# Attention stage: the copies of the transposed probabilities from PSUM to SBUF move from VectorE to ScalarE

## What is computed

```python
# x: (16, 2048, 1024), D_K = 128, D_FF = 4096
xn = _layernorm(x)
Q, K, V = xn @ Wq, xn @ Wk, xn @ Wv
logits = Q K^T * D_K ** (-0.5)          # causal mask above the diagonal: -inf
attn = softmax(logits)
a = (attn @ V) @ Wo
hidden = xn @ W1 + b1
q = hidden + (cos(th)*wr + sin(th)*wi) * (wi*sin(th + hidden*0.1)) * 0.1
f = relu(q) @ W2 + b2
x + a + f
```

## Time and profile before

| | |
|---|---|
| median of 2 runs | 1229.64 us (1228.83 to 1230.45) |
| profiled execution | 1230.11 us |
| its span on the slowest core (core 6), first to last instruction | 1228.5 us |
| spans of the eight cores | 1222.5 to 1228.5 us |
| busy: PE, ACT, DVE | 88%, 48%, 37% of the span |
| attention stage, first sequence | 71.9 to 132.9 us of the span |
| attention stage, second sequence | 192.6 to 267.4 us |
| FFN stage | from 268 us to the end; from 268 to 1225 us PE is busy for 928.9 of 957 us |
| the 80 copies L591 on DVE | 48.9 us busy |

### The profile page before, as it was taken

The page is one execution under the profiler, slowest core; times in us unless marked ns, Lnnn a source line. Parts: engine busy times, 40 slices in busy tenths (PEclk is TensorE's granted clock), DMA queues, the critical chain, the costliest instruction groups (busy, mean ns, idle before and its releaser), DMA issues.

```text
span 1228.5 us, 23871 instructions; the slowest of 8 cores (1222.5 to 1228.5 us)
## 1 busy us (share of the span) xinstructions
PE 1084.7 (88%) x7936; PEld 733.9 (60%) x7936; DVE 452.8 (37%) x1007; ACT 595.5 (48%) x1285; POOL 37.0 (3%) x48
## 2 busy tenths in 40 slices
PE   1767474769999999999999999999999999999998
PEld 1644373446566656665666566656665666566665
DVE  3626553643333333333333333333333333333333
ACT  2955494445454544454445444544454445444444
POOL 1310021000000000000000000000000000000000
PEclk9968686789999999999999999999999999999999
DMA  7889578920202020202020202020202020202000
GB/s 166 252 139 170 159 228 142 176 87 1 77 11 86 1 87 1 87 1 86 2 86 2 86 1 87 1 86 2 86 1 87 1 87 1 86 1 87 20 33 35
DMA packets 47416, 87.13 MB, mean 71 GB/s; under 512 B 7106, under 2 KB 23490, under 8 KB 46274
## 3 DMA queue, kind: packets, MB, share of 16 engines
q1 hardware_dynamic: 36226, 59.39, 15.8%
q0 software_dynamic: 11072, 26.22, 11.6%
HBM read 78.25 MB, written 25.17 MB: 84 GB/s over the span
## 4 chain that ended last, share of the span: by engine, by line
PE 72%; DVEq 2%; DVE 2%; issue 1%; ACT 1%; ACTq 0%
PE psOut L832 37%; PE psW L806 36%; DVEq L752 2%; DVE probs L754 1%; ACT rb_sb L779 1%; DVE u_sb L731 1%; DVE out_sb L754 0%; ACT L771 0%; DVEq L759 0%; DVEq L730 0%; ACT ss_sb L771 0%; DVEq L751 0%; DVEq L728 0%; ACTq L778 0%; ACTq L776 0%
## 5 line engine op out<-in xcount | busy, mean ns | idle before, releaser
L832 PE MATMUL psOut<-W_sb,rb_sb 128*128 128x512 bf16 x2048 | 532.5, 383 | 10.8 <-ACT rb_sb L779 10.8
L806 PE MATMUL psW<-xn_r,W_sb 128*128 128x256 bf16 x4096 | 537.5, 275 | 1.5 <-PEq L386 1.5
L806 PEld LDWEIGHTS psW<-xn_r,W_sb 128*128 128x128 bf16 x4096 | 404.0, 99 | 161.7 <-issue 6.2
L731 DVE SCALAR_TENSOR_TENSOR u_sb<-ss_sb,Rp_sb,psW 128x256 f32<-128x256 bf16 x512 | 244.2, 479 | 584.5 <-ACT ss_sb L771 571.2
L771 ACT ACTIVATE ss_sb<-psW,phb_sb 128x256 bf16<-128x256 f32 x512 | 242.4, 474 | 445.3 <-PE psW L806 445.3
L832 PEld LDWEIGHTS psOut<-W_sb,rb_sb 128*128 128x128 bf16 x2048 | 200.8, 99 | 151.8 <-issue 20.9
L779 ACT ACTIVATE rb_sb<-u_sb,b_sb 128x256 bf16<-128x256 f32 x511 | 254.5, 498 | 57.1 <-DVE u_sb L731 55.1
L591 DVE CAST pT_big<-psT 128x512 bf16<-128x512 f32 (+2 forms) x80 | 48.9, 612 | 38.6 <-PE psT L526 34.0
L370 PE MATMUL psTx<-diag_li,probs 128*128 128x128 bf16 x176 | 15.5, 239 | 41.0 <-DVE diag_li L274 40.8
L526 PE MATMUL psT<-diag_li,xn_rg 128*128 128x128 bf16 x272 | 31.8, 264 | 22.2 <-DVE pT_big L591 15.6
L540 PE MATMUL psO<-pT_big,V_tm 128*128 128x128 bf16 x272 | 30.8, 253 | 17.7 <-DVE pT_big L591 16.7
(11 more groups left out here) (92 smaller groups left out, 429.5 us busy)
## 6 DMA issues: line engine op xcount, KB each, us to landing
x_sb<-x SPq DMA_DIRECT2D x52, 512.0 KB, 6.0
W_sb<-w POOLq DMA_DIRECT2D x8, 2048.0 KB, 40.7
xn_scr<-xn_rg POOLq DMA_DIRECT2D x32, 256.0 KB, 4.3
xn_r<-xn_scr SPq DMA_DIRECT2D x16, 512.0 KB, 7.5
out<-out_sb SPq DMA_DIRECT2D x32, 256.0 KB, 3.1
out<-probs SPq DMA_DIRECT2D x32, 256.0 KB, 5.3
xn_r<-x SPq DMA_DIRECT2D x12, 512.0 KB, 6.4
Q_fm<-b2rep SPq DMA_DIRECT2D x1, 512.0 KB, 3.7
```

What stands on the lines that cost most here:

```text
L731: su2.inc(v.scalar_tensor_tensor(u2_sb[ci % 2][:], ss_sb[ci % 2][:], Rp_sb[:, c:c + 1], psW1[slot][:], ALU.mult, ALU.add))
L806: ins = t.matmul(psW1[slot][:], W1_sb[:, k * DFF + c * 128: k * DFF + (c + 1) * 128], xn_r3[g % 2][:, k * R3:(k + 1) * R3], start=(k == 0) ...
L832: ins = t.matmul(psOut[tt][:, h * 512:(h + 1) * 512], rb_sb[cw % 3][:, tt * 128:(tt + 1) * 128], W2_sb[:, cc * D + h * 512: cc * D + (h + ...
```

## The change

The copies leave DVE's loop and enter ACT's. On ACT they stand behind the exponentials of tile qi and ahead of the copy of psO, with the same waits but with no drain ahead of each. Their semaphores are the same. PE's program is unchanged.

```diff
@@ vector engine, attention stage
                         se2.inc(ins)
-                        for si in range(nsg[j]):
-                            b = bank_of[(j, si)]
-                            v.wait_ge(stx2.h, stx2_b + cum_sg[j] + si + 1)
-                            if j >= 1:
-                                v.wait_ge(spv.h, spv_b + j)
-                            v.drain()
-                            w = segw2(j, si)
-                            (st2e if b == 0 else st2eV).inc(v.tensor_copy(
-                                pT_big[si // 2][:, (si % 2) * 512:(si % 2) * 512 + w],
-                                psT2[b][:, 0:w]))
                         for fn in pv.get(j, []):
                             fn(v)
@@ scalar engine, attention stage (qq is the query tile, j = qq - 1)
                                 se1.inc(ins)
+                        if j >= 0:
+                            for si in range(nsg[j]):
+                                b = bank_of[(j, si)]
+                                sc.wait_ge(stx2.h, stx2_b + cum_sg[j] + si + 1)
+                                if j >= 1:
+                                    sc.wait_ge(spv.h, spv_b + j)
+                                w = segw2(j, si)
+                                (st2e if b == 0 else st2eV).inc(sc.copy(
+                                    pT_big[si // 2][:, (si % 2) * 512:(si % 2) * 512 + w],
+                                    psT2[b][:, 0:w]))
                         j2 = qq - 1
```

## The result

| | before | after |
|---|---|---|
| median of the runs beside each other | 1231.18 us (14 runs) | 1234.86 us (15 runs) |
| ratio after / before | | 1.0035, 95% interval 1.0026 to 1.0044 |
| span of the slowest core in the profile | 1228.5 us | 1235.0 us |

A forecast was written before the change was run, and what follows sets the result against it. It took a chain of handovers, with no engine full, to bound the attention stages. First sequence +5.6, second -2.0 and clock +2 on 1230.1 gave 1235.7, stated as 1235 us; range 1231 to 1239 (0.62), eight in ten 1227 to 1243.

The forecast's parts named there:

- Copies are late by the second exponential: First sequence, large tiles: copies on ACT start only after the next tile's second exponential; whole first sequence +5.6 us.
- the term for the place: First sequence, tiles 11 to 14: copies queued behind the exponentials lengthen the steps by +4.0 us in sum.
- A pitch of 0.47 us: Copies on ACT: successive 512-column copies start 0.47 us apart, against some 0.75 us on DVE.
- The two ACT copies of the earlier trace: Existing ACT copies of the same shape, type and memories, taken as the model: 0.60 us each, pitch 0.47.
- The bound of +6 us for a longer pitch: Copies on ACT: a pitch of 0.60 + 0.15 us instead of 0.47 would add +0.25 in some 24 steps, +6.
- Second sequence: diag_li early: Without copies DVE makes diag_li sooner; tiles 2 to 7 change by -3.6 us, the whole second sequence by -2.0.
- The stall is given back: Second sequence, tile 14: ACT's 4.2 us wait before the arctangent goes, but tile 13's later copies give it back almost whole.
- The clock, +2 us within 0 to 7: Attention stages, nine large steps: sparser PE work lowers its granted clock; +2 us taken, 7 if all fall, 0 if none.
- The faster copy wins: Rival, attention stages: shorter copies and vanished waits save 25 us, giving 1205; chance 0.02 whole, 0.13 for a mild gain.
- The clock stays low: Rival, tiles 9 to 15 of both stages: 0.8 us a tile, 7 in all, giving 1240.7; chance 0.18.
- a term that I had at 0: Layer norm stage between the two attention stages: forecast difference 0.

The follow-up runs named there:

- e3: Changed kernel, but for query tiles 8 to 15 the copies stand on ACT between the two exponentials; ratio to before 0.9969.
- e10: Kernel before, copies on DVE, but in the first sequence each tile's copies wait for the next tile's exponentials; ratio to before 1.0142.
- e8: Changed kernel with 12 unused matmuls on idle PE ahead of the third segment's transposes of tiles 8 to 15; ratio to before 0.9992.
- e4: Changed kernel with a drain put ahead of each copy on ACT, as DVE had; ratio to before 1.0102.
- e6: Kernel before with only DVE's step L460 of tile 13 moved ahead of that tile's copies; ratio to before 0.9970.

## Why the prediction was right

The measured 1234.86 us lies beside the 1235 forecast. The nearness is in part luck: the forecast was built on two runs of before with a median of 1229.64 us, and the median of the 14 runs is 1231.18. The difference was forecast as 5.6 us (5.4 from that median) and is 4.3 (3.2 to 5.4). The mechanism, late copies in the first sequence and earlier diag_li in the second, is as forecast. Point by point, by medians of the cores (medians of single steps do not add up exactly to the median of a stage):

- **Copies are late by the second exponential.** Right. Tile 12's first copy starts at its end (113.74) to the hundredth, and e3 and e10 show that the place is the cause. The steps of tiles 8 to 10 grew by 0.5, 0.6 and 0.0 us (+1.4 forecast for the three, 1.1 measured) and small tiles by +0.2 in all (+0.3). Tiles 11 to 14 grew by 4.8 us in all where the term for the place was 4.0; with the gaps filled (e8), at the clock of before (0.96 against 0.95), they grow by 2.9. So the place alone was put too high by about 1 us there, and the clock adds 1.9. The step of tile 12 on core 6 was to be near 5.1 us and is 5.43; the logits at 1.2 GHz make the difference and more.
- **A pitch of 0.47 us.** Right, 0.48; DVE's, put at 0.75, is 0.78. Since ACT's copies overlap, all 80 add 38.3 us to its busy time on core 6 and not 43. The two ACT copies of the earlier trace rows were the right neighbours. The bound of +6 us for a longer pitch was too small: with a drain (pitch 0.67), which also delays each first copy, it is 11 us (e4).
- **Second sequence: diag_li early.** Right to 0.1 us: tiles 2 to 7 (with the sliver of tiles 0 and 1) are 3.6 us shorter, as forecast. Tiles 8 to 11 came to +0.5 (0.5 forecast), 12 and 13 to +2.8 (2.0), 14 and the last to -1.8 (-0.9); the last two misses cancel.
- **The stall is given back.** Right. Two table loads and two exponentials now stand ahead of tile 13's copies; the step went from 8.94 to 8.74, and e6 shows the 3.7 us that could be had.
- **The clock, +2 us within 0 to 7.** Right in kind. e8 gets 4.0 us back in the two stages. That is more than the change itself lost by the clock, most likely: over the whole stages the granted clock, median of the cores, fell from 0.68 and 0.67 to 0.67 and 0.64 by the change, and the filling raised it to 0.75, above that of before.
- **The rivals.** "The faster copy wins" needs copies that do not wait for the exponentials. They did wait (e10), and of its 25 us (14.6 of them at 0.26 us a copy, where the two pitches of the prediction differ by 0.28) only the 3.6 of the small tiles in the second sequence, 0.2 at the arctangent and the shorter pitch came about. "The clock stays low" is a part of the truth and not the whole.
- **What no step foresaw**: the layer norm stage between the two, 0.8 to 1.4 us longer by the means over twelve profiles, 2.5 in the first pair.

The parts add up to what the timed runs give (3.2 to 5.4): +5.5 and -2.6 us from the attention stages and 0.8 to 1.4 from the layer norm stage make 3.7 to 4.3. The agreement is loose, since one profile of the first stage is good to about 2 us. The hit of the total owes something to luck here too: the attention stages alone gave 3 us where I had 5.6, and a term that I had at 0 filled a good part of the difference. Of that 5.6 the part for the clock, +2, showed in tiles 11 to 14 of the first sequence and not in the stages as a whole, because the kernel before was at the low level in tiles 8 to 10. After the change tile 10 had the higher clock of the two, and its step did not grow. My rows were of core 6, where the kernel before was at the high level from 101 us on; on that core the first stage grew by 6.7 us and not by the median's 5.5.

What stays open is why the layer norm stage is longer.

## What to carry to other kernels

Before work is moved to another engine, look at what stands ahead of it in that engine's queue at the moment when its input is ready: here a copy 17% shorter made each large step about 1 us longer, because it stood behind an exponential that nobody was waiting for yet. The first place to look for a gain is therefore the order within a queue (L460 ahead of the copies: 3.7 us for three lines; copies ahead of the second exponential: 8 us against after), and the second a split of the same work by who is free when each piece is ready. A wait that vanishes from the profile is worth only what does not queue up behind its other causes.

## What was not expected of the hardware

- Useless matmuls in idle gaps made the kernel faster: 12 of them, of 128 columns each, in each of tiles 8 to 15 raised the granted clock of the stages from 0.65 - 0.67 to 0.72 - 0.76 on core 6, and the step of tile 14 in the first sequence fell from 6.2 to 5.4 us (median of the cores).
- A drain ahead of a copy on ACT costs 0.18 to 0.19 us, also ahead of the first one behind an exponential (e4); between two of ACT's instructions without one, the second starts when the first's time ends, or up to 0.1 us earlier (a pitch of 0.48 for copies of 0.58).
- From the end of ACT's exponential to a DVE copy that waited for it were 0.38 us in e10, the accumulator's read and DVE's drain included; a copy on ACT itself started at the exponential's end.
